# A selective-scan kernel: the softplus correction moves from GpSimd to TensorE, row statistics from VectorE to ScalarE

## The chip, the core and the metric

One core of a Trainium2 chip runs the whole kernel. It has four compute engines that run side by side, each with its own instruction stream: TensorE (PE: matmuls, with PEld for the weight loads), VectorE (DVE), ScalarE (ACT) and GpSimd (POOL); SyncE (SP) here only issues DMAs. Engines wait for each other by semaphores. Inside an engine the order is fixed: an instruction that waits holds up all behind it. SBUF is the on-chip memory, PSUM the memory into which TensorE writes; GpSimd doesn't touch PSUM in this kernel. The metric is the device time of one execution in microseconds; a run of this kernel can tell about 0.2% from no change.

## The reference, cut to what matters

Input x is 8 batches of 512 tokens of width 256. The first half is a selective scan (a Mamba block) with residual and norms; the second half is a shared and a routed feed-forward layer with 8 experts.

```
x   = x + layernorm(ssm(layernorm(x)))
h   = layernorm(x) * norm_w + norm_b ;  h = h @ in_proj_w.T        # 512 channels
h   = silu(conv4(h))                    # 4 taps along time
dt  = softplus(proj[..., :1] @ dt_proj_w.T + dt_proj_b)            # proj = h @ x_proj_w.T
state = exp(A * dt_t) * state + B_t * x_t      # 16 states per channel, 512 steps of time
y   = sum over states of state * C_t  + D * x_t
out = silu(y) @ out_proj_w.T + x
x   = x + layernorm(shared_ffn(n) + routed_ffn(n)),  n = layernorm(x)
```

The softplus is computed as max(z, 0) + log(1 + u) with u = exp(-|z|). With w = 1 + u rounded, and then w - 1, the kernel has the rounded u in the tile lt; log(1 + lt) is compared with lt. The difference lt - log(1 + lt), called the loss, plus a margin of 2e-9, is cut at (0.707 u)^2 by a minimum. The time step is dt = max(z, 0) + u - minimum.

## The kernel before

**Layout.** 512 channels are 4 chunks of 128 partitions (C = 4), each with 512 tokens in the free dimension. Two chunks are a half (H = 2), so one scan works on a tile of 128 x 1024 of one state, and a batch has Q = 32 scans: 16 states for each of two halves.

**A round.** Round i (the iteration function of each engine) handles the scans of batch i, and between them, at given steps q of the 32, the front of batch i+1 (norm, input projection, convolution, Silu, projections, dt), the back of batch i-1 (output projection, residual, norms, router matmuls), and the lead of batch i+2 (the statistics of x). Nothing but the code's order of each engine and the semaphores set when a thing runs.

**A step q.** ScalarE writes the decays exp(A dt) for scan q+2 into PSUM (tile psX, two halves of 128x511, L763, ring of 2). The input product bx = x * B comes from GpSimd for even q (L500, issued four steps ahead, from B rows spread over the partitions by DMA) or from VectorE for odd q (L1078); for VectorE TensorE spreads the B row over the partitions with one matmul into the bank psB (spread_b, L1486), two steps ahead. Step 22 is an exception, its product is VectorE's. VectorE scans (L1090). GpSimd multiplies the state by C (L511, 'weigh'). TensorE sums the weighted states of step q-3 into psY (total, L1529). psB is one bank: a spread must wait until VectorE has read the one before.

**The front's dt part, by steps.** 10: ScalarE's Silu with a table load before and one behind (L660, L610), 11 to 14: projections on TensorE, the dt row on ScalarE, 14 to 17: |z|, exp, 1 + u, minus 1 on ScalarE (L673, L676, L679, L682), 18: ScalarE copies y out of PSUM (keep_y, L753). 19: the logarithm (L685). 20: GpSimd's lt minus logarithm (L516, 128x2048). 22: ScalarE's square (L688). 23 and 24: VectorE's minimum in two halves (L1039, 128x1024 each, both operands in SBUF). 25 to 28: for each chunk three matmuls by plus or minus identity add relu(z), u and the minimum in the bank psF (L1433 to L1435), and ScalarE copies the sum to dt (L694); one bank serves all, so the next sum waits for the copy.

**The back, by steps.** 15 and 17: output projection (L1451), 16 and 18: residual on VectorE (L1048), 19: router matmuls of batch i-2 (choose, L1476), 22 and 24: second residual (L1058), 25: statistics, 29 and 30: transposes (L1467). **The lead.** Step 10: VectorE takes the statistics of x of batch i+2 (L1006, four bn_stats, and L1010) into mv0; steps 29 to 31: ScalarE makes scale and bias of them and norms x. The statistics are copied at step 8 for the back of the same batch.

Before round 0 a function first_front handles batch 0 alone, and it is not changed. Round 7 has no front and no lead.

## Time and profile before

| | |
|---|---|
| time, median of 3 runs | 1411.01 us (1410.88 to 1412.58) |
| the profiled execution's own time | 1411.09 us |
| its span, first to last instruction | 1409.3 us |
| mean granted TensorE clock | 0.94 |
| PE busy | 1175.4 us (83%) |
| DVE busy | 1089.8 us (77%) |
| ACT busy | 770.9 us (55%) |
| POOL busy | 1088.4 us (77%) |

The scans run from 51.7 to about 989 us, then come the tail of the last batch, the shared layer and the routed layer. The busy shares of the table are means over all of that; the change lies in the scan stage alone, and what a piece of it is worth has to be read there, in one round. In the page's 40 slices, TensorE's granted clock is 0.8 to 0.9 of full speed in the scan stage, and 0.9 behind it.

### The profile page before, as it was taken

The numbers are of one execution on the slowest core, as the hardware profiler recorded it, in microseconds if no ns is written. First come the engines' busy times: TensorE is split into PE (matmuls) and PEld (weight loads), VectorE is DVE, ScalarE is ACT, GpSimd is POOL, SyncE is SP. The second block draws the span as 40 slices with busy tenths as digits, with TensorE's granted clock in tenths as the row PEclk, the third lists the DMA queues.
The fourth block names the chain that finished last, engine by engine and source line by source line (L and its number), as shares of the span: only waits on it lengthen the run. The fifth ranks groups of instructions, "written<-read, shape, count | busy, mean of one in ns | idle before, by whom it ended". The sixth has DMA issues, their size and how long they took to land.

```text
span 1409.3 us, 15754 instructions
## 1 busy us (share of the span) xinstructions
PE 1175.4 (83%) x4782; PEld 518.5 (37%) x4783; DVE 1089.8 (77%) x1449; ACT 770.9 (55%) x1275; POOL 1088.4 (77%) x565
## 2 busy tenths in 40 slices
PE   5667678787886987888789688788999999999996
PEld 2222223222321422322233142233556655566653
DVE  3599999999999999999999989799241115776675
ACT  5757468676876866867686686556431111111111
POOL 0489999999999999999999999999122814444553
PEclk9898899999899999989998999999999999999998
DMA  3921211240150122014015012300269522222220
GB/s 108 274 68 62 90 60 32 75 150 0 65 192 1 62 91 106 32 75 149 1 66 175 1 62 90 134 0 31 90 238 324 162 71 82 81 81 79 83 67 15
DMA packets 72075, 127.71 MB, mean 91 GB/s; under 512 B 8759, under 2 KB 48448, under 8 KB 67904
## 3 DMA queue, kind: packets, MB, share of 16 engines
q1 hardware_dynamic: 60432, 103.72, 22.2%
q0 software_dynamic: 7152, 16.81, 3.7%
q10 hardware_dynamic: 4416, 6.29, 1.3%
q8 instruction: 33, 0.54, 0.2%
q14 instruction: 42, 0.34, 0.1%
HBM read 97.79 MB, written 31.76 MB: 92 GB/s over the span
## 4 chain that ended last, share of the span: by engine, by line
PE 36%; POOL 29%; issue 15%; DVE 12%; ACT 8%; DMA 0%; POOLq 0%; ACTq 0%; SPq 0%; DVEq 0%
POOL state L511 18%; PE psX L1647 10%; POOL bx L500 9%; DVE state L1090 6%; PE psX L1582 5%; PE psY L1595 3%; PE psY L1664 2%; PE bank L1664 2%; PE psY L1529 2%; PE bank L1451 2%; POOL lt L516 2%; ACT psX L763 2%; PE bank L1486 1%; DVE bx L1078 1%; DVE acc L1025 1%
## 5 line engine op out<-in xcount | busy, mean ns | idle before, releaser
L511 POOL TENSOR_TENSOR state<-state,cbc 128x1024 f32<-128x1024 f32 x256 | 606.6, 2398 | 14.9 <-DVE state L1090 14.8
L1090 DVE TENSOR_TENSOR_SCAN state<-psX,bx 128x1024 f32<-128x1024 f32 x256 | 578.5, 2279 | 38.5 <-ACT psX L763 23.1
L763 ACT ACTIVATE psX<-dt,aneg 128x511 f32<-128x511 f32 x512 | 330.7, 679 | 199.0 <-DVE state L1090 197.6
L500 POOL TENSOR_TENSOR bx<-xh,bbc 128x1024 f32<-128x1024 f32 x120 | 291.1, 2426 | 59.5 <-DMA bbc<-bc_rows 43.1
L1529 PE MATMUL psY<-state,ident 64*64 64x512 f32 x2048 | 287.5, 654 | 20.3 <-POOL state L511 20.0
L1486 PE MATMUL bank<-prow,ident 128*128 128x512 f32 x272 | 169.9, 710 | 113.3 <-DVE bx L1078 113.3
L1078 DVE TENSOR_TENSOR bx<-xh,bank 128x1024 f32<-128x1024 f32 x136 | 162.7, 1196 | 7.7 <-PE bank L1486 7.6
L1529 PEld LDWEIGHTS psY<-state,ident 64*64 64x64 f32 x2048 | 63.9, 140 | 206.8 <-issue 126.2
L961 ACT ACTIVATE sg<-psX 128x512 f32<-128x512 f32 x39 | 23.3, 597 | 196.5 <-PE psX L1647 196.5
L1486 PEld LDWEIGHTS bank<-prow,ident 128*128 128x128 f32 x272 | 48.0, 209 | 206.9 <-DVE bx L1078 166.9
L581 POOL DMA_INDIRECT ysl<-shared_rows,idx x39 | 40.3, 1033 | 80.6 <-DVE idx L1258 75.9
L1167 DVE TENSOR_TENSOR actS<-sg,psX 128x512 f32<-128x512 f32 x28 | 19.0, 686 | 103.6 <-ACT sg L911 103.6
L1647 PE MATMUL psX<-wg,xsT 128*128 x156 | 77.2, 617 | 1.3 <-DVE xsT L1243 0.6
L1647 PE MATMUL psX<-wu,xsT 128*128 x156 | 73.3, 592 | 0.0
L1406 PE MATMUL bank<-lt,win 128*128 128x512 f32 x112 | 55.5, 618 | 15.7 <-DVE acc L1025 14.4
L590 POOL DMA_INDIRECT result<-yo,idx x39 | 40.1, 1029 | 36.8 <-DVE yo L1306 29.3
L1025 DVE SCALAR_TENSOR_TENSOR acc<-bank,cw,acc 128x511 f32<-128x511 f32 (+2 forms) x84 | 62.3, 742 | 3.3 <-ACT acc L654 1.2
L561 POOL COPY xrow<-ids 128x4 f32<-128x4 f32 x8 | 1.6, 203 | 77.6 <-issue 55.1
L1249 DVE TENSOR_TENSOR actN<-sg,psX 128x512 f32<-128x512 f32 x39 | 26.8, 688 | 44.1 <-ACT sg L961 41.6
L1451 PE MATMUL bank<-wout,yv 128*128 128x256 f32 x256 | 58.5, 381 | 2.0 <-ACT yv L709 1.9
L911 ACT ACTIVATE sg<-psX 128x512 f32<-128x512 f32 x28 | 16.5, 596 | 76.8 <-PE psX L1582 76.8
L1582 PE MATMUL psX<-xg,shg 128*128 128x512 f32 x112 | 53.1, 596 | 1.8 <-DVE actS L1167 1.8
(200 smaller groups left out, 1718.8 us busy)
## 6 DMA issues: line engine op xcount, KB each, us to landing
cbc<-bc_rows SPq DMA_DIRECT2D x32, 1024.0 KB, 5.0
bbc<-bc_rows SPq DMA_DIRECT2D x16, 1024.0 KB, 6.2
slot_in<-ao SPq DMA_DIRECT2D x1, 5011.5 KB, 35.1
xsl<-slot_in SPq DMA_DIRECT2D x39, 128.5 KB, 2.0
xin<-in_x SPq DMA_DIRECT2D x8, 512.0 KB, 4.5
xr<-in_x SPq DMA_DIRECT2D x8, 512.0 KB, 5.5
x_rows<-ao SPq DMA_DIRECT2D x8, 512.0 KB, 2.9
xn_rows<-xr SPq DMA_DIRECT2D x8, 512.0 KB, 3.2
```

What stands on the lines that cost most here:

```text
L500: nc.gpsimd.tensor_tensor(bx[q % RB][:], xh[par][:, h * CH:(h + 1) * CH], bbc[:, n // 2].unsqueeze(1).broadcast_to([P, CH, L]), ALU.mult). ...
L511: nc.gpsimd.tensor_tensor(w[:], w[:], cbc[:, n].unsqueeze(1).broadcast_to([P, CH, L]), ALU.mult).then_inc(weighted, 1)
L763: e = nc.scalar.activation(decay[q % RD][:, c, 1:L], dt[par][:, h * CH + c, 1:L], ACT.Exp, scale=aneg[:, h * CH + c, n:n + 1])
L1025: last = nc.vector.scalar_tensor_tensor(out=acc[:, c, m:L], in0=psF[:, 0:L - m], scalar=cw[:, c, TAPS - 1 - m:TAPS - m], in1=acc[:, c, m:L ...
L1078: nc.vector.tensor_tensor(bx[q % RB][:], xh[par][:, h * CH:(h + 1) * CH], psB[:].unsqueeze(1).broadcast_to([P, CH, L]), ALU.mult).then_inc ...
L1090: nc.vector.tensor_tensor_scan(st[q % RS][:].rearrange("p c t -> p (c t)"), decay[q % RD].rearrange("p c t -> p (c t)"), bx[q % RB][:].rea ...
L1451: last = nc.tensor.matmul(psF[:, (j % 2) * DIM:(j % 2 + 1) * DIM], yv[:, c, j * P:(j + 1) * P], wout[:, c], start=(c == 0), stop=(c == C - 1))
L1486: nc.tensor.matmul(psB[:], ident[:, n:n + 1].broadcast_to([P, P]), prow[par][:], start=True, stop=True).then_inc(b_bcast, 1)
L1529: done = nc.tensor.matmul(psY[o * HP:(o + 1) * HP, r], weights(half, c), src[half, c], start=first, stop=last_)
L1582: last = nc.tensor.matmul(bank, w[:, k, c * P:(c + 1) * P], xg[g % 2][:, k], start=(k == 0), stop=(k == KC - 1))
L1647: last = nc.tensor.matmul(bank, xsT[i][:, k], w[:, bass.ds(ereg[i], 1), k].rearrange("p a n -> p (a n)"), start=(k == 0), stop=(k == KC - 1))
L1664: last = nc.tensor.matmul((psF, psG)[i][:, 0:DIM], actT[i][:, c], wd[:, bass.ds(ereg[i], 1), c].rearrange("p a n -> p (a n)"), start=(c == ...
```

## The change

**Loss.** GpSimd's subtraction is gone. TensorE makes it, chunk by chunk, at steps 19, 21, 23 and 25 (LOSS_AT), in the chunk order 2, 3, 0, 1 (LOSS_ORDER): two matmuls into psB, identity by lt and minus identity by the logarithm. VectorE's minimum comes behind the scan of the same step, as four instructions of 128x512 that read psB, and each spread of B that stood at these steps now stands one step later, behind the wait for the minimum. ScalarE's logarithm moves from step 19 to 18 in two halves, the upper chunks' into the tile yv; the square is split in two (steps 19 and 21), and Relu moves from 23 to 22. The dt sums take the chunks in the new order.

**Products.** Step 22's product goes to GpSimd, which has 16 of 32 now.

**Statistics of x.** VectorE's lead is gone from the loop. ScalarE makes them with eight passes over 256 columns that sum up along the row: four sums at steps 3 to 6, the mean and the first sum of squares at step 7, three more at step 9. Each pass waits for the one before. The copy of the statistics moves from step 8 to 6.

The pieces of the diff, in the order of the file: the constants, GpSimd's subtraction, ScalarE's lead and front, VectorE's minimum and its lead in the loop, TensorE's loss and its loop.

```diff
-    BY_POOL = [q % 2 == 0 and q not in (22,) for q in range(Q)]
+    BY_POOL = [q % 2 == 0 for q in range(Q)]
+    LOSS_AT = (19, 21, 23, 25)
+    LOSS_ORDER = (2, 3, 0, 1)
...
-            def loss(f, par):
-                pool.wait_ge(soft_ready, f + 1)
-                nc.gpsimd.tensor_tensor(lt[:], lt[:], dt[par][:], ALU.subtract).then_inc(loss_ready, 1)
...
             def lead(f, par, q):
+                def row_pass(k, func, bias, dst):
+                    if k == 0:
+                        act.wait_ge(mv0_ready, f)
+                    else:
+                        act.wait_ge(row_passes, (2 * J - 1) * (f - 2) + k)
+                    nc.scalar.activation(unused[:], xin[:, k % J, :], func, bias=bias,
+                                         accum_out=dst).then_inc(mv0_ready if k == 2 * J - 1 else row_passes, 1)
+                if q in (3, 4, 5, 6):
+                    j = q - 3
+                    if j == 0:
+                        act.wait_ge(x_loaded, 16 * (f + 1))
+                    row_pass(j, ACT.Identity, 0.0, xsum[:, j:j + 1])
+                if q == 7:
+                    act.wait_ge(row_passes, (2 * J - 1) * (f - 2) + J)
+                    nc.scalar.activation(mv0[par][:, :, 0], xsum[:], ACT.Identity,
+                                         scale=-1.0 / DIM).then_inc(mean_ready, 1)
+                    act.wait_ge(mean_ready, f - 1)
+                    row_pass(J, ACT.Square, mv0[par][:, 0, 0:1], mv0[par][:, 0, 1:2])
+                if q == 9:
+                    for j in range(1, J):
+                        row_pass(J + j, ACT.Square, mv0[par][:, j, 0:1], mv0[par][:, j, 1:2])
...
+                if q == 18:
+                    act.wait_ge(lt_ready, f + 1)
+                    if not (isinstance(f, int) and f == 1):
+                        act.wait_ge(oproj_ready, 2 * (f - 1))
+                    nc.scalar.activation(yv[:, CH:C], lt[:, CH:C], ACT.Ln, bias=1.0)
+                    nc.scalar.activation(dt[par][:, 0:CH], lt[:, 0:CH], ACT.Ln, bias=1.0).then_inc(soft_ready, 1)
                 if q == 19:
-                    act.wait_ge(lt_ready, f + 1)
-                    nc.scalar.activation(dt[par][:], lt[:], ACT.Ln, bias=1.0).then_inc(soft_ready, 1)
+                    nc.scalar.activation(dt[par][:, CH:C], tmp[:, CH:C], ACT.Square, scale=HALF_ROOT).then_inc(sq_ready, 1)
+                if q == 21:
+                    act.wait_ge(loss_made, C * (f - 1) + 2)
+                    nc.scalar.activation(yv[:, CH:C], tmp[:, 0:CH], ACT.Square, scale=HALF_ROOT).then_inc(sq_ready, 1)
...
-                if q in (23, 24):
-                    h = slice(0, 2) if q == 23 else slice(2, 4)
-                    dve.wait_ge(loss_ready, f + 1)
-                    dve.wait_ge(sq_ready, f + 1)
-                    nc.vector.scalar_tensor_tensor(out=lt[:, h], in0=lt[:, h], scalar=LN_MARGIN, in1=dt[par][:, h],
+                if q in LOSS_AT:
+                    k = LOSS_AT.index(q)
+                    c = LOSS_ORDER[k]
+                    dve.wait_ge(loss_made, C * (f - 1) + k + 1)
+                    if c < CH:
+                        dve.wait_ge(sq_ready, 2 * f + 1)
+                        square = yv[:, CH + c]
+                    else:
+                        dve.wait_ge(sq_ready, 2 * f)
+                        square = dt[par][:, c]
+                    nc.vector.scalar_tensor_tensor(out=lt[:, c], in0=psB[:], scalar=LN_MARGIN, in1=square,
                                                    op0=ALU.add, op1=ALU.min).then_inc(min_done, 1)
...
-                    if do_lead:
-                        lead(i + 2, par, q)
...
+            def loss(f, par, q):     
+                k = LOSS_AT.index(q)
+                c = LOSS_ORDER[k]
+                logarithm = dt[par][:, c] if c < CH else yv[:, c]
+                pe.wait_ge(soft_ready, f + 1)
+                pe.wait_ge(dve_bx, (f - 1) * DQ + NTH_D[q + 1])
+                nc.tensor.matmul(psB[:], ident[:], lt[:, c], start=True, stop=False)
+                nc.tensor.matmul(psB[:], minus[:], logarithm, start=False, stop=True).then_inc(loss_made, 1)
...
                 for q in range(Q):
-                    if not BY_POOL[(q + 2) % Q]:
+                    if do_front and q - 1 in LOSS_AT:
+                        pe.wait_ge(min_done, 2 + C * i + LOSS_AT.index(q - 1) + 1)
+                        spread_b(i, par, q + 1)
+                    if do_front and q in LOSS_AT:
+                        loss(i + 1, 1 - par, q)
+                    elif not BY_POOL[(q + 2) % Q]:
```

TensorE before, steps 17 to 21 of a round that has all parts: the second output projection and the sum of step 14 open it; `bank<-prow` is a spread of B, `psY<-xh,dD` the skip term.

```order
L1486 MATMUL bank<-prow,ident 128x512
L1451 MATMUL bank<-wout,yv 128x256 x8
L1529 MATMUL psY<-state,ident 64x512 x8
L1486 MATMUL bank<-prow,ident 128x512
L1529 MATMUL psY<-xh,dD 64x512 x4
L1529 MATMUL psY<-state,ident 64x512 x4
L1476 MATMUL bank<-gw,xnTb 128x8 x8
L1486 MATMUL bank<-prow,ident 128x512
L1529 MATMUL psY<-state,ident 64x512 x4
L1486 MATMUL bank<-prow,ident 128x512
```

And in the changed kernel, from the spread of step 17 on (L1533 is the spread, L1524 and L1525 the loss, L1489 the output projection, L1514 the router, L1576 the sums):

```order
L1533 MATMUL bank<-prow,ident 128x512
L1489 MATMUL bank<-wout,yv 128x256 x8
L1576 MATMUL psY<-state,ident 64x512 x8
L1524 MATMUL bank<-lt,ident 128x512
L1525 MATMUL bank<-yv,minus 128x512
L1576 MATMUL psY<-xh,dD 64x512 x4
L1576 MATMUL psY<-state,ident 64x512 x4
L1514 MATMUL bank<-gw,xnTb 128x8 x8
L1533 MATMUL bank<-prow,ident 128x512
L1576 MATMUL psY<-state,ident 64x512 x4
L1524 MATMUL bank<-lt,ident 128x512
```

The spread of step 21 stood ahead of the skip term and the router; now the two loss matmuls stand there, and the spread has gone behind the router.

TensorE before, from the last spread of the minimum's stretch: the spread of step 27, the sum of step 22 and the first dt sum.

```order
L1486 MATMUL bank<-prow,ident 128x512
L1529 MATMUL psY<-state,ident 64x512 x4
L1433 MATMUL bank<-acc,ident 128x512
L1434 MATMUL bank<-tmp,ident 128x512
L1435 MATMUL bank<-lt,minus 128x512
L1529 MATMUL psY<-state,ident 64x512 x4
L1433 MATMUL bank<-acc,ident 128x512
L1434 MATMUL bank<-tmp,ident 128x512
L1435 MATMUL bank<-lt,minus 128x512
L1486 MATMUL bank<-prow,ident 128x512
```

And now (L1471 to L1473 are the dt sums):

```order
L1524 MATMUL bank<-lt,ident 128x512
L1525 MATMUL bank<-dt,minus 128x512
L1576 MATMUL psY<-state,ident 64x512 x4
L1471 MATMUL bank<-acc,ident 128x512
L1472 MATMUL bank<-tmp,ident 128x512
L1473 MATMUL bank<-lt,minus 128x512
L1533 MATMUL bank<-prow,ident 128x512
L1576 MATMUL psY<-state,ident 64x512 x4
L1471 MATMUL bank<-acc,ident 128x512
```

The loss stands in the place of the spread of step 27, and that spread is between the first and the second dt sum.

VectorE before, from scans 19 and 20 to scan 24 (L1078 the products, L1039 the first half of the minimum):

```order
L1090 SCALAR_TENSOR_TENSOR state<-psX,bx 128x1024 x2
L1078 TENSOR_TENSOR bx<-xh,bank 128x1024
L1090 SCALAR_TENSOR_TENSOR state<-psX,bx 128x1024
L1078 TENSOR_TENSOR bx<-xh,bank 128x1024
L1090 SCALAR_TENSOR_TENSOR state<-psX,bx 128x1024
L1078 TENSOR_TENSOR bx<-xh,bank 128x1024
L1058 TENSOR_TENSOR ao<-bank,xr 128x512
L1090 SCALAR_TENSOR_TENSOR state<-psX,bx 128x1024
L1039 SCALAR_TENSOR_TENSOR lt<-lt,dt 128x1024
L1090 SCALAR_TENSOR_TENSOR state<-psX,bx 128x1024
```

And now, from scan 19 on (L1129 the scans, L1117 the products, L1078 the minimum of one chunk):

```order
L1129 SCALAR_TENSOR_TENSOR state<-psX,bx 128x1024
L1078 SCALAR_TENSOR_TENSOR lt<-bank,dt 128x512
L1129 SCALAR_TENSOR_TENSOR state<-psX,bx 128x1024
L1117 TENSOR_TENSOR bx<-xh,bank 128x1024
L1129 SCALAR_TENSOR_TENSOR state<-psX,bx 128x1024
L1078 SCALAR_TENSOR_TENSOR lt<-bank,dt 128x512
L1129 SCALAR_TENSOR_TENSOR state<-psX,bx 128x1024
L1117 TENSOR_TENSOR bx<-xh,bank 128x1024
L1097 TENSOR_TENSOR ao<-bank,xr 128x512
L1129 SCALAR_TENSOR_TENSOR state<-psX,bx 128x1024
L1078 SCALAR_TENSOR_TENSOR lt<-bank,yv 128x512
```

A minimum stands behind scan 19 already, between it and scan 20, and of the three products in a row that of step 22 is gone. Scans are printed as SCALAR_TENSOR_TENSOR here.

## Rows read from the trace of the kernel before

**Rows 1.** Busy time by engine in round 4: us, busy (x instructions), PEclk, DMA share, GB/s.
```profile
528.90:646.00 117.10, 96.53 (x423) 34.81 (x418) 109.88 (x95) 85.28 (x142) 113.88 (x48) 0.91 0.22 77
```

**Rows 2.** Timeline, DVE: start, us, line, out<-in, [idle before <-releaser]; two scans 0.
```profile
528.90 2.29 DVE L1090 TENSOR_TENSOR_SCAN state<-psX,bx 128x1024 f32<-128x1024 f32 x1 [1.46 <-ACT psX L763]
...
646.03 2.29 DVE L1090 TENSOR_TENSOR_SCAN state<-psX,bx 128x1024 f32<-128x1024 f32 x1 [1.25 <-ACT psX L763]
```

**Rows 3.** Groups by line: xcount | busy us, mean ns | idle before, releaser.
```profile
L511 POOL TENSOR_TENSOR state<-state,cbc 128x1024 f32<-128x1024 f32 x256 | 606.6, 2398 | 14.9 <-DVE state L1090 14.8
...
L763 ACT ACTIVATE psX<-dt,aneg 128x511 f32<-128x511 f32 x512 | 330.7, 679 | 199.0 <-DVE state L1090 197.6
...
L516 POOL TENSOR_TENSOR lt<-lt,dt 128x2048 f32<-128x2048 f32 x7 | 31.8, 4540 | 0.0
...
L1025 DVE SCALAR_TENSOR_TENSOR acc<-bank,cw,acc 128x511 f32<-128x511 f32 (+2 forms) x84 | 62.3, 742 | 3.3 <-ACT acc L654 1.2
...
L631 ACT ACTIVATE lt<-xin,nmr,rstd 128x256 f32<-128x256 f32 x32 | 17.1, 588 | 0.1
...
L1006 DVE BATCH_NORM_STATS2 bst<-xin 128x6 f32<-128x256 f32 x32 | 11.2, 414 | 3.7 <-DMA xin<-in_x 3.7
```

**Rows 4.** Timeline, POOL, steps 16 to 19 of round 4.
```profile
592.88 7.03 POOL L511 TENSOR_TENSOR state<-state,cbc 128x1024 f32<-128x1024 f32 x3
602.84 2.36 POOL L511 TENSOR_TENSOR state<-state,cbc 128x1024 f32<-128x1024 f32 x1 [2.92 <-DVE state L1090]
```

**Rows 5.** Timeline, DVE: scans 13 and 14, and the residual sum of step 16.
```profile
578.28 4.47 DVE L1090 TENSOR_TENSOR_SCAN state<-psX,bx 128x1024 f32<-128x1024 f32 x2 [0.69 <-ACT psX L763]
...
591.65 0.69 DVE L1048 TENSOR_TENSOR ao<-bank,ao 128x512 f32<-128x512 f32 x1 [2.02 <-PE bank L1451]
```

**Rows 6.** Timeline, ACT: decays of step 10, copy of y, logarithm.
```profile
569.31 1.30 ACT L763 ACTIVATE psX<-dt,aneg 128x511 f32<-128x511 f32 x2 [3.10 <-DVE state L1090]
...
599.95 1.08 ACT L753 ACTIVATE yv<-psY 128x512 f32<-128x512 f32 x2
...
604.03 1.90 ACT L685 ACTIVATE dt<-lt 128x2048 f32<-128x2048 f32 x1
```

**Rows 7.** Timeline, DVE: products of steps 21 and 25, second half of the minimum.
```profile
604.86 1.20 DVE L1078 TENSOR_TENSOR bx<-xh,bank 128x1024 f32<-128x1024 f32 x1
...
619.84 1.19 DVE L1078 TENSOR_TENSOR bx<-xh,bank 128x1024 f32<-128x1024 f32 x1
...
621.55 1.77 DVE L1039 SCALAR_TENSOR_TENSOR lt<-lt,dt 128x1024 f32<-128x1024 f32 x1
```

**Rows 8.** Timeline, PE: step 19, then the spread of step 27 and a dt sum.
```profile
599.81 1.12 PE L1486 MATMUL bank<-prow,ident 128*128 128x512 f32 x2
601.17 1.09 PE L1529 MATMUL psY<-xh,dD 64*64 64x512 f32 x8 [0.24 <-ACT yv L753]
...
603.05 1.95 PE L1476 MATMUL bank<-gw,xnTb 128*128 128x8 f32 x16
...
621.09 2.07 PE L1486 MATMUL bank<-prow,ident 128*128 128x512 f32 x2 [3.26 <-DVE bx L1078]
...
624.78 1.13 PE L1433 MATMUL bank<-acc,ident 128*128 128x512 f32 x2
```

**Rows 9.** Busy time by engine behind that idle stretch, columns as in rows 1.
```profile
621.00:625.00 4.00, 3.92 (x11) 1.03 (x12) 4.00 (x4) 0.45 (x1) 4.00 (x2) 0.57 0.37 131
```

**Rows 10.** Timeline of round 0: ACT's copy of y, DVE's first half minimum.
```profile
127.77 1.06 ACT L753 ACTIVATE yv<-psY 128x512 f32<-128x512 f32 x2
...
142.04 8.26 DVE L1039 SCALAR_TENSOR_TENSOR lt<-lt,dt 128x1024 f32<-128x1024 f32 x1 [1.13 <-ACT dt L688]
```

**Rows 11.** Round 0: landing of x, issued at 63.03; ACT's decays of step 4.
```profile
63.03 4.00 SPq L362 DMA_DIRECT2D xin<-in_x  x1
...
DMA to landing us min/median/max: 15.3/15.3/15.3
...
74.47 1.30 ACT L763 ACTIVATE psX<-dt,aneg 128x511 f32<-128x511 f32 x2 [3.11 <-DVE state L1090]
```

More of the change, by code:

```diff
@@ L123, in build @@
         mv0 = [sb(f"mv0_{i}", [P, J, 2], where=A) for i in range(2)]
+        xsum = sb("xsum", [P, J], where=A)
+        unused = sb("unused", [P, DIM], BF16, where=A)
         mv = [sb(f"mv{i}", [P, J, 2], where=A) for i in range(3)]
@@ L240, in build @@
         mv0_ready = sem("mv0_ready")
+        row_passes = sem("row_passes")
+        mean_ready = sem("mean_ready")
         mv_ready = [sem(f"mv_ready{i}") for i in range(3)]
@@ L525, in iteration @@
                     weigh(i, q)
-                    if do_front and q == 20:
-                        loss(i + 1, 1 - par)
             for q in range(0, RB, 2):
@@ L759, in decays @@
                     act.wait_ge(scanned, i * Q + q - RD + 1)
-                if n == 0:
-                    act.wait_ge(dt_ready, C * i + CH * (h + 1))
+                if n == 0 and isinstance(i, int) and i == 0:
+                    act.wait_ge(dt_ready, CH * (h + 1))
+                elif n == 0:
+                    act.wait_ge(dt_ready, C * (i + 1))
                 for c in range(CH):
@@ L1423, in front @@
                 if q in (25, 26, 27, 28):
-                    c = q - 25
+                    k = q - 25
+                    c = LOSS_ORDER[k]
                     pe.wait_ge(relu_ready, f + 1)
-                    pe.wait_ge(min_done, 2 * f + c // 2 + 1)
-                    if c:
-                        pe.wait_ge(dt_ready, C * f + c)
+                    pe.wait_ge(min_done, 2 + C * (f - 1) + k + 1)
+                    if k:
+                        pe.wait_ge(dt_ready, C * f + k)
                     else:
```

30 lines of the change are left out of this document (17 added, 13 removed).

## The prediction, made before the changed kernel had run

> **What bounds the kernel now.** I read the page first, then the busy times of one round, then the timelines of VectorE, ScalarE and TensorE through it. A round is one pass of the 32-step loop of one batch; a step q is one scan of a state. Round 4 runs from scan 0 at 528.90 to the next scan 0 at 646.03 us, 117.1 us [rows 2]. In it GpSimd is busy 113.9, VectorE 109.9, TensorE 96.5 and ScalarE 85.3 us, at a granted clock of 0.91 [rows 1]. GpSimd looks like the bound, and the change takes work from it. Its own sum: 32 weightings and 15 products at 2.31 us from start to start (three in a row take 7.03 [rows 4]; the mean of one is 2.40 with the overlap [rows 3]) are 108.6, the 128x2048 subtraction 4.5 [rows 3], so 113.1, 4 less than the round. And it waits: at step 19 for 2.92 us, for the scan [rows 4]. A bound engine doesn't wait once a round. I therefore take VectorE's row of work for what sets the round, with the waits in it for ScalarE and TensorE: 0.69 us before scan 13 for its decays, 2.02 before the residual sum of step 16 for TensorE [rows 5], 1.25 before the next scan 0 [rows 2]. The question is then what becomes of those waits and whether new ones come in.
>
> **The statistics of x leave VectorE (step 10).** Four bn_stats at 0.41 us [rows 3] and the small operations behind them are about 1.7 us. What comes next on VectorE is scans 11 and 12, the product of step 13 and scan 13, and scan 13 waits for ScalarE, which has since the end of scan 10 made decays 12, loaded a table, done both Silus and loaded the table back, from 569.31 on [rows 6]; the old 0.69 us wait is the end of that. With the 1.7 us gone, scan 13 still starts at 578.3 and the wait is 2.4. The same chain runs on through the dt row, the projections and the output projection to the residual sum at 591.65, 22.3 us behind scan 10, with 2.02 us of waiting left over there too [rows 5, 6]. So I cost this part at zero, not at -1.7 (bounds -1.7 and 0).
>
> **Its replacement on ScalarE.** Eight passes over 256 columns, each waiting for the one before: 0.59 us each by the pass of the same shape over the same tile [rows 3], 4.7 us and two small ones. No row has such a pass with an accumulated sum; the bounds are the row itself and, as an estimate, twice it, 1.2. I take 0.6, the nearer row. They stand in steps 3 to 7 and 9, where ScalarE idles before its decays: 3.10 us before those of step 10 [rows 6], where three passes go in (1.9), and 199 us over the kernel's 512 decay halves, nearly all waiting for a scan [rows 3]. Zero, up to +0.5 a round at 1.2 us each. One exception: x must now be there at step 3. In round 0 its load is issued at 63.03 and lands 15.3 us later, at 78.3, beside the 5 MB of zeros; ScalarE's next decays were at 74.47 [rows 11] and have the second convolution tap behind them, for which VectorE is then late. About +3 us, once.
>
> **The product of step 22 goes to GpSimd.** VectorE saves 1.2 to 1.4 us. GpSimd takes the 2.3 in the gap before step 19's scan [rows 4], which covers it.
>
> **The loss goes from GpSimd to TensorE.** This is the dear part. TensorE, in order, now does at step 19: two matmuls of 512 columns into psB, the weighted sum of step 16, the router's matmuls; and only at step 20, after VectorE's minimum has read psB, the spread of B for step 21. Before, that spread was first of all. When can the first matmul start? Both logarithms must be done. ScalarE's copy of y out of PSUM, which stays ahead of them, ends at 601.0 [rows 6]; two half-size logarithms of 0.95 each (half of the whole one's 1.90, same group) end at 602.9. TensorE has been free since about 599.9, where it now has the spread [rows 8]. Two matmuls at about 1.0 (an identity matmul at the high clock is 1.13 alone, and overlaps with the next [rows 8]): 605.0. Scan 19 ended at 602.7, as GpSimd's start behind it tells [rows 4], so VectorE stands 2.4 us. The minimum, from PSUM, is 0.66 start to start (0.74 each by the convolution's form [rows 3]). Behind the two matmuls TensorE has the sum of step 16 with its skip term, 1.9 (601.17 to 603.05), the router 1.95 and the spread 1.0 [rows 8], to 610.0. The product of step 21, which started at 604.86 [rows 7], starts at 610.1: +5.2. From there VectorE goes product, scan, minimum (the loss of the next chunk runs under the scan), so its row to the product of step 25 is: saved 1.4 (step 22) and the old first minimum with its wait 1.7, added two minima 1.3. That product starts at 623.2 or 623.3 instead of 619.84 [rows 7]: +3.4.
>
> Then the last loss and the four sums. Behind the product of step 25 TensorE had one spread and a weighted sum, 3.7 us from 621.09 to the first of the dt sums at 624.78, at the low clock [rows 8]; now two matmuls and that sum, 3.0 at the high one. That is -0.7. The spread of step 27 now stands between the first and the second dt sum: +1.0. ScalarE copies each sum, and the last copy, the transposes and the norm's small operations release the decays of the next scan 0; this is what the 1.25 us wait is the end of [rows 2]. VectorE's shorter second minimum (1.77 to 0.66, [rows 7]) lies beside it. Net +0.3. A round at the high clock: +3.4 +0.3, with 0.2 to 0.4 of semaphore times, **+4.1**.
>
> **The clock.** In rows: TensorE idled 3.26 us before 621.09, and its next matmul took 2.07 instead of 1.13 [rows 8]; the granted clock in that stretch was 0.57, so mostly 1.2 GHz [rows 9]. In the changed kernel it idles from 599.9 to 602.9, nearly as long, ahead of matmuls for which VectorE stands. Cold they cost +2.0, and the sum and router behind them +1.3: +3.3. I take half of that. The Trainium skill, TensorE: Matmul & The Clock Gate, section HAM oscillation, says that an array left without work for long enough goes back to the low clock, so that what follows the wait starts slow, every round. That rule counts the whole of it.
>
> **Sum.** Rounds 2 to 6: 5 x 4.1 = 20.5. Round 1 has no router matmuls ahead of the spread: 4.1 - 2.0 = 2.1. Round 0: its first minimum took 8.26 us after 1.13 of waiting [rows 10], where a later one took 1.77 [rows 7], with GpSimd busy beside both; the new form reads one operand from PSUM, as the convolution does, whose 84 instructions have a mean of 0.74 [rows 3], so that goes; but the first loss waits till 132.8 (copy of y to 128.8 [rows 10], 1.9, 1.95) against scan 19's end at 127.4. By the same walk the step 25 scan is about 6 us earlier and the dt chain gives back 3; with x's 3 us: 0. Round 7 has no front: it lost the step 22 product from VectorE (-1.4), GpSimd gains 2.3 but enters with less in arrears: -1. Together +21.6 warm; six rounds of half the clock's 3.3 are +10: about +31 less a little. Against the profiled execution's 1411.09 us (span 1409.3, 1.8 around it, and the median of the runs 1411.01) that is **1441 us**.
>
> **The rivals.** (a) *GpSimd is the bound after all* (faster). By its row a round goes from 113.1 and two delays of 1.0 by the old minima to 48 x 2.31 = 110.9, -4.2; seven rounds -29, +2.3 in the last: 1384. For it: 113.9 busy of 117.1 [rows 1]; the Trainium skill, SBUF — State Buffer, section SBUF: two separate sides, adds that a VectorE operation with two SBUF inputs takes a port pair that GpSimd shares, so the old minima, and not the new ones, would hold it up. Against it: the 2.92 us wait [rows 4], and that no VectorE wait names GpSimd. It needs the loss to be ready when scan 19 ends, 2.4 us earlier than I find; part of it, with the step 22 product and stats saved and psB's turn hidden, would give 1390 to 1405. (b) *Cold TensorE* (slower than forecast): 3.3 at the first loss in six rounds and as much as 2.9 before the dt sums (3.26 us of idle led to that before): 21.6 + 20 + 17 = +58, 1469. This is also where the skill's clock rule points: the first of the two alone gives 1411 + 21.6 + 20 = 1453. (c) *The moves cancel*: the router and the weighted sum turn out to lie under VectorE's scans, and +5.2 shrinks to about the 2.4 of the wait, while 1.2, 1.0 and 0.7 come back: -0.5 to +1 a round, 1408 to 1416. (d) *The statistics don't hide*: 1.2 us passes push the decays before both Silus and the whole chain by 0.5 to 1 us a round, +4 to +7 on any of the others.
>
> **How the numbers follow.** Forecast with its neighbours (1424 to 1456): 0.54. Cold (b), above 1456: 0.19. (c): 0.08, half of it within 0.2%, which is 2.8 us and about what runs of this kernel can tell. (a): 0.19. So faster by over 0.2% has 0.20, within 0.04, slower 0.76. The range should leave out at most 2 in 10: from 1400 (a part of (a) stays out) to 1468 (the end of (b)). The likeliest case alone: 1424 to 1456.
>
> **What would show it.** Right: no bn_stats of x on VectorE, and scan 13 waiting about 2.4 us for ScalarE; VectorE idle 2 to 4 us before the first of the four minima, released by TensorE, and again before the product of step 21; GpSimd idle several us more in every round; 121 to 124 us from scan 0 to scan 0 in rounds 2 to 6. Wrong: the first minimum starting right behind scan 19; scan 13 moving up with the statistics gone, which would give 1.7 us a round that I give nothing for; GpSimd without a gap and rounds of 111 to 114 us, which is rival (a); or rounds of 117.

## The result, and the profile after

The changed kernel takes **1433.9 us** (median of 4 runs, 1432.7 to 1435.2) against 1411.6 (4 runs, 1410.9 to 1412.6): ratio **1.0157, 95% interval 1.0144 to 1.0170**. It is slower, as forecast, by 22 us in place of 30. The profiled execution took 1433.3 us.

The page of the changed kernel, its span, its busy times and the shares of its chain:

```profile
span 1431.2 us, 16057 instructions
...
PE 1203.3 (84%) x4878; PEld 533.3 (37%) x4879; DVE 1060.0 (74%) x1401; ACT 796.9 (56%) x1393; POOL 1064.5 (74%) x566
...
PE 48%; ACT 20%; DVE 20%; issue 10%; DMA 1%; DVEq 0%; ACTq 0%; POOLq 0%; POOL 0%; SPq 0%
```

The chain is the work that ended last, followed back from the end of the kernel. In the page of the kernel before its shares were:

```profile
PE 36%; POOL 29%; issue 15%; DVE 12%; ACT 8%; DMA 0%; POOLq 0%; ACTq 0%; SPq 0%; DVEq 0%
```

GpSimd and VectorE have each lost work (24 and 30 us), and the kernel is slower. In the chain GpSimd's share is 0% where it was 29%. Round 4, columns as in [rows 1]:

```profile
539.90:661.60 121.70, 100.06 (x443) 36.92 (x440) 106.62 (x87) 89.73 (x161) 111.23 (x49) 0.94 0.22 75
```

It is 4.6 us longer than before [rows 1], with 3.3 us less on VectorE and 2.6 less on GpSimd. So waits grew. Where, the starts of the scans tell, in us from the round's scan 0, read from VectorE's timeline of both traces (the columns are scans):

| round 4 | 13 | 17 | 19 | 20 | 21 | 23 | 25 | 28 | 31 | next 0 |
|---|---|---|---|---|---|---|---|---|---|---|
| before | 49.4 | 63.4 | 71.6 | 73.8 | 77.3 | 84.9 | 94.3 | 104.0 | 113.6 | 117.1 |
| after | 49.2 | 63.2 | 71.4 | 77.6 | 83.7 | 90.4 | 97.1 | 107.4 | 118.2 | 121.7 |

To scan 19 nothing has moved. Scan 20 is 3.8 later, scan 21 is 6.4 later; by scan 25 it has given back 3.6 of that, and 1.8 come back on before scan 0. VectorE's timeline at these places (start, us, line, out<-in, and in brackets the idle before it and its releaser):

```profile
589.12 4.47 DVE L1129 TENSOR_TENSOR_SCAN state<-psX,bx 128x1024 f32<-128x1024 f32 x2 [2.12 <-ACT psX L793]
...
602.49 0.69 DVE L1087 TENSOR_TENSOR ao<-bank,ao 128x512 f32<-128x512 f32 x1 [2.01 <-PE bank L1489]
...
611.34 2.26 DVE L1129 TENSOR_TENSOR_SCAN state<-psX,bx 128x1024 f32<-128x1024 f32 x1
...
616.90 0.69 DVE L1078 SCALAR_TENSOR_TENSOR lt<-bank,dt 128x512 f32<-128x512 f32 x1 [3.30 <-PE bank L1525]
617.51 2.28 DVE L1129 TENSOR_TENSOR_SCAN state<-psX,bx 128x1024 f32<-128x1024 f32 x1
...
622.19 1.22 DVE L1117 TENSOR_TENSOR bx<-xh,bank 128x1024 f32<-128x1024 f32 x1 [2.40 <-PE bank L1533]
...
661.63 2.29 DVE L1129 TENSOR_TENSOR_SCAN state<-psX,bx 128x1024 f32<-128x1024 f32 x1 [1.24 <-ACT psX L793]
```

Scan 13 and the residual sum of step 16 start where they started, 0.69 [rows 5] having become 2.12 before the first of them. The two new waits, 3.30 for the first loss and 2.40 for the spread behind it, are 5.7 us. The wait for scan 0 is the old one [rows 2]. ScalarE at steps 18 and 19: the copy of y, then the two logarithms, which end at 613.76:

```profile
610.79 1.08 ACT L781 ACTIVATE yv<-psY 128x512 f32<-128x512 f32 x2
611.76 1.06 ACT L710 ACTIVATE yv<-lt 128x1024 f32<-128x1024 f32 x1
612.70 1.06 ACT L711 ACTIVATE dt<-lt 128x1024 f32<-128x1024 f32 x1
```

TensorE from there:

```profile
608.77 1.95 PE L1576 MATMUL psY<-state,ident 64*64 64x512 f32 x16
613.81 1.25 PE L1524 MATMUL bank<-lt,ident 128*128 128x512 f32 x2 [3.09 <-ACT dt L711]
614.85 1.91 PE L1525 MATMUL bank<-yv,minus 128*128 128x512 f32 x2
616.69 1.76 PE L1576 MATMUL psY<-xh,dD 64*64 64x512 f32 x8
618.28 1.03 PE L1576 MATMUL psY<-state,ident 64*64 64x512 f32 x8
619.24 1.95 PE L1514 MATMUL bank<-gw,xnTb 128*128 128x8 f32 x16
621.05 1.10 PE L1533 MATMUL bank<-prow,ident 128*128 128x512 f32 x2
```

TensorE idles 3.09 us until the logarithms end; the second loss matmul and the skip term take 1.91 and 1.76 where the same kinds take 1.02 and 1.09 elsewhere; then the router, and the spread last. The clock granted in such a stretch differs from round to round. Busy times by engine, the PEclk third from the end, of the six us from 73 us behind scan 0, in rounds 1, 3 and 4:

```profile
250.15:256.15 6.00, 5.69 (x16) 1.94 (x20) 2.04 (x3) 2.49 (x4) 2.35 (x1) 0.50 0.75 220
492.20:498.20 6.00, 4.67 (x28) 2.07 (x28) 3.65 (x3) 3.44 (x5) 2.54 (x2) 1.00 0.68 203
612.90:618.90 6.00, 5.09 (x20) 1.51 (x20) 2.70 (x3) 3.02 (x4) 2.35 (x1) 0.72 0.69 217
```

It is 1.00 in round 3 (and 5), 0.72 in round 4 (and 2 and 6), where part of the stretch went at 1.2 GHz, and 0.50 in round 1, where all of it did. The idle time ahead of it is 3.1 us in all of these rounds. Round 1 has both loss matmuls slow, and its skip term took 1.99:

```profile
250.46 2.07 PE L1524 MATMUL bank<-lt,ident 128*128 128x512 f32 x2 [3.09 <-ACT dt L711]
252.32 1.92 PE L1525 MATMUL bank<-yv,minus 128*128 128x512 f32 x2
```

In round 0, where TensorE idled 9.9 us, the two took 2.07 and 1.92 as well. VectorE's wait for the first loss follows the clock: 3.96 us in round 1, 3.26, 3.30 and 2.66 in rounds 2, 4 and 6, 2.35 in rounds 3 and 5.

GpSimd, off the path, now waits more: 0.96 and 3.83 us at steps 19 to 21, where before it waited 2.92 once [rows 4]. Summed over the kernel (the waits: waiter, releaser, us, times, longest), its products waited for VectorE 16.4 us before and now:

```profile
POOL bx L507 <- DVE state L1129: 63.3, 41, 5.7
```

By rounds, scan 0 to scan 0, in us:

| round | 0 | 1 | 2 | 3 | 4 | 5 | 6 |
|---|---|---|---|---|---|---|---|
| before | 125.3 | 116.7 | 116.9 | 118.3 | 117.1 | 118.1 | 115.8 |
| after | 125.2 | 120.2 | 121.9 | 120.7 | 121.7 | 120.5 | 119.8 |
| difference | -0.1 | +3.5 | +5.0 | +2.4 | +4.6 | +2.4 | +4.0 |

The sum is +21.8. In rounds 2 to 5 the differences alternate, and so do the rounds of both kernels: before, 3 and 5 are the long ones, and after, 2 and 4. In the kernel before, the low clock reached further into the dt sums in round 3 than in round 4 (same columns, 9.5 us from 94.5 us behind scan 0):

```profile
505.10:514.60 9.50, 9.50 (x30) 3.10 (x22) 9.27 (x14) 3.68 (x6) 9.50 (x5) 0.82 0.35 132
623.40:632.90 9.50, 9.50 (x38) 2.91 (x30) 9.27 (x13) 4.58 (x11) 9.50 (x5) 0.94 0.37 136
```

There the kernel before loses its time too: from scan 28 to scan 31 it takes 10.7 and 10.8 us in rounds 3 and 5, and 9.4 and 9.6 in rounds 2 and 4. In the changed kernel the clock over the dt sums is 1.00 in all rounds. Round 7 to the start of its last scan is 106.7 in both, and what follows from there takes 422.7 before and 422.6 after.

### The profile page after: what moved, and what is told of

Its sections match the earlier page's. It is cut to its first block, busy times and chain, and to the rows that moved or that the text cites. A ratio compares the mean times of both kernels' runs of the same rounds, so it can differ in the third digit from the quotient of the medians.

```text
span 1431.2 us, 16057 instructions
## 1 busy us (share of the span) xinstructions
PE 1203.3 (84%) x4878; PEld 533.3 (37%) x4879; DVE 1060.0 (74%) x1401; ACT 796.9 (56%) x1393; POOL 1064.5 (74%) x566
## 4 chain that ended last, share of the span: by engine, by line
PE 48%; ACT 20%; DVE 20%; issue 10%; DMA 1%; DVEq 0%; ACTq 0%; POOLq 0%; POOL 0%; SPq 0%
PE psX L1699 10%; DVE state L1129 10%; ACT psX L793 5%; PE psY L1576 5%; PE psX L1634 5%; PE bank L1533 3%; DVE bx L1117 3%; DVE acc L1060 3%; PE psY L1647 3%; PE psY L1716 2%; PE bank L1716 2%; PE bank L1471 2%; PE bank L1456 2%; PE bank L1473 2%; PE bank L1472 2%
## 5 line engine op out<-in xcount | busy, mean ns | idle before, releaser
L1129 DVE TENSOR_TENSOR_SCAN state<-psX,bx 128x1024 f32<-128x1024 f32 x256 | 579.4, 2281 | 50.7 <-ACT psX L793 33.1
L518 POOL TENSOR_TENSOR state<-state,cbc 128x1024 f32<-128x1024 f32 x256 | 599.3, 2365 | 14.7 <-DVE state L1129 14.7
L507 POOL TENSOR_TENSOR bx<-xh,bbc 128x1024 f32<-128x1024 f32 x128 | 303.4, 2371 | 106.6 <-DVE state L1129 63.3
L1576 PE MATMUL psY<-state,ident 64*64 64x512 f32 x2048 | 273.9, 629 | 1.2 <-POOL state L518 1.2
L1533 PE MATMUL bank<-prow,ident 128*128 128x512 f32 x256 | 152.5, 680 | 70.5 <-DVE bx L1117 68.6
L1117 DVE TENSOR_TENSOR bx<-xh,bank 128x1024 f32<-128x1024 f32 x128 | 153.4, 1198 | 22.7 <-PE bank L1533 22.5
L1576 PEld LDWEIGHTS psY<-state,ident 64*64 64x64 f32 x2048 | 63.2, 137 | 178.1 <-issue 148.5
L1533 PEld LDWEIGHTS bank<-prow,ident 128*128 128x128 f32 x256 | 44.1, 201 | 149.3 <-DVE bx L1117 99.3
L1524 PE MATMUL bank<-lt,ident 128*128 128x512 f32 x56 | 33.0, 672 | 48.4 <-ACT dt L711 28.5
L1489 PE MATMUL bank<-wout,yv 128*128 128x256 f32 x256 | 58.5, 381 | 1.0 <-ACT yv L737 0.9
```

The source lines that it names most:

```text
L507: nc.gpsimd.tensor_tensor(bx[q % RB][:], xh[par][:, h * CH:(h + 1) * CH], bbc[:, n // 2].unsqueeze(1).broadcast_to([P, CH, L]), ALU.mult). ...
L518: nc.gpsimd.tensor_tensor(w[:], w[:], cbc[:, n].unsqueeze(1).broadcast_to([P, CH, L]), ALU.mult).then_inc(weighted, 1)
L1117: nc.vector.tensor_tensor(bx[q % RB][:], xh[par][:, h * CH:(h + 1) * CH], psB[:].unsqueeze(1).broadcast_to([P, CH, L]), ALU.mult).then_inc ...
L1129: nc.vector.tensor_tensor_scan(st[q % RS][:].rearrange("p c t -> p (c t)"), decay[q % RD].rearrange("p c t -> p (c t)"), bx[q % RB][:].rea ...
L1489: last = nc.tensor.matmul(psF[:, (j % 2) * DIM:(j % 2 + 1) * DIM], yv[:, c, j * P:(j + 1) * P], wout[:, c], start=(c == 0), stop=(c == C - 1))
L1533: nc.tensor.matmul(psB[:], ident[:, n:n + 1].broadcast_to([P, P]), prow[par][:], start=True, stop=True).then_inc(b_bcast, 1)
```

## The experiments

Theory: VectorE's row of work, with the waits in it for ScalarE and TensorE, sets the round; the loss at step 19 stands in that row, and nothing else of the change costs or gives anything there. Rivals: GpSimd's total sets it; or the pieces taken from VectorE had been worth something, and a larger cost hides that. Ratios are against the kernel before. Round times are from each run's one profiled execution.

### One part alone, on the kernel before

**The statistics of x alone** (ScalarE's eight passes in, the bn_stats out, as in the change's diff).

> The kernel before with only the statistics of x moved to ScalarE. Theory (VectorE's row with the ScalarE chain that starts behind scan 10 sets the round): the 1.7 us that leave step 10 come back as a wait before scan 13 (0.69 to 2.4 us); each round keeps its length, and round 0 grows by up to 3 us because ScalarE waits for x: 1411 to 1415. Rival (VectorE's busy time is what counts): 1.7 us in six rounds, 1401.

1408.4 us (10 runs, 1406.6 to 1414.2), 0.9987 [0.9973, 1.0000]. Rounds 1 to 6 are 117.1, 117.6, 118.2, 117.4, 118.0 and 115.7, 704.0 in sum against 702.9: as before, although VectorE has 1.7 us less in each. Scan 13 of round 4 waits 2.12 here too:

```profile
581.77 4.47 DVE L1121 TENSOR_TENSOR_SCAN state<-psX,bx 128x1024 f32<-128x1024 f32 x2 [2.12 <-ACT psX L789]
```

So this part is worth zero in the loop, as costed. Round 0 was 127.5, +2.2, for the later x. The runs lie in two groups, about 1408 (six) and 1414 (four); the profiled one, with its one stall in round 0, is of the upper. What parts them isn't shown. The 6 us between them are near what such a stall costs (below), but no run of the lower group has a profile.

**Step 22's product alone.**

```diff
-    BY_POOL = [q % 2 == 0 and q not in (22,) for q in range(Q)]
+    BY_POOL = [q % 2 == 0 for q in range(Q)]
```

> The kernel before with only the product of step 22 moved to GpSimd. Theory: VectorE's 1.4 us turn into a longer wait before the first half of the minimum, which hangs on GpSimd's subtraction and ScalarE's square; GpSimd's 2.3 us go into its gap before step 19: 1409 to 1412. Rival 1 (GpSimd is the bound): 2.3 us in eight rounds, 1429. Rival 2 (VectorE's work is the bound without the chain): -1.4 in eight, 1400.

1428.9 us (4 runs), **1.0125** [1.0108, 1.0142]: a miss, and a large one. The number is the one that "GpSimd is the bound" gave, but the rounds are not: four of rounds 1 to 6 take 117.2 to 118.7, and rounds 3 and 6 take 125.6 and 123.9. Those two are 15.4 of the 18 us, round 0 is another 2.6. In rounds 3 and 6 the first half of the minimum (L1039, both operands in SBUF) is stuck:

```profile
501.34 8.26 DVE L1039 SCALAR_TENSOR_TENSOR lt<-lt,dt 128x1024 f32<-128x1024 f32 x1 [2.48 <-ACT dt L688]
...
862.90 8.25 DVE L1039 SCALAR_TENSOR_TENSOR lt<-lt,dt 128x1024 f32<-128x1024 f32 x1 [3.29 <-ACT dt L688]
```

GpSimd beside the first of them:

```profile
501.50 2.42 POOL L500 TENSOR_TENSOR bx<-xh,bbc 128x1024 f32<-128x1024 f32 x1
503.81 4.71 POOL L511 TENSOR_TENSOR state<-state,cbc 128x1024 f32<-128x1024 f32 x2
```

VectorE began at 501.34, GpSimd's next instruction at 501.50; GpSimd ran three instructions in a row, to 508.52, and VectorE ended at 509.60, 1.1 us behind them. The 14 of its kind take 1.34 us at the least and 1.77 in the median. The kernel before has one such stall, in round 0 [rows 10], and this one has that too. In a round without it the meeting is the same, but it is GpSimd whose instruction is the longer one, 3.36 us in place of some 2.4 (the kernel before, round 1):

```profile
263.86 1.36 DVE L1039 SCALAR_TENSOR_TENSOR lt<-lt,dt 128x1024 f32<-128x1024 f32 x1 [0.64 <-ACT dt L688]
...
264.06 3.36 POOL L500 TENSOR_TENSOR bx<-xh,bbc 128x1024 f32<-128x1024 f32 x1
```

The start doesn't tell the two cases apart. In the kernel before, in the one with the statistics alone and in this one there are 21 first halves of the minimum; all began 0.25 to 0.28 us ahead of the end of the GpSimd instruction then running, and 5 were stuck. What decides isn't in these traces. The change's minima read one operand from PSUM, and none is stuck, here or in the eight kernels below that are made from it, 252 minima in all (source line: count, min/median/max in ns, first and last start):

```profile
L1078 DVE SCALAR_TENSOR_TENSOR lt<-bank,dt x14: 666/678/692, 136.9 to 867.5; 128x512 f32<-128x512 f32 x14
L1078 DVE SCALAR_TENSOR_TENSOR lt<-bank,yv x14: 657/666/669, 149.5 to 882.6; 128x512 f32<-128x512 f32 x14
```

In the undisturbed rounds scan 23 was 1.3 us earlier and scan 25 where it had been: with step 22's product gone, the minimum waits for ScalarE's square instead (its waits for it went from 3.8 us to 18.0). So the product is worth nothing to the old order, and with it gone the stall strikes in two more rounds.

**Most of GpSimd's subtraction left out** (only the first token of each chunk is subtracted, in 0.22 us in place of 4.54).

```diff
-    nc.gpsimd.tensor_tensor(lt[:], lt[:], dt[par][:], ALU.subtract)
+    nc.gpsimd.tensor_tensor(lt[:, :, 0:1], lt[:, :, 0:1], dt[par][:, :, 0:1], ALU.subtract)
```

> The kernel before with GpSimd's subtraction done for one column of each chunk only (the rest of it is left out), 4.5 us less GpSimd work a round. Theory: GpSimd isn't the bound; only VectorE's 0.3 us wait for the minimum goes, and in round 0 a part of its 8.3 us minimum: 1402 to 1410. Rival (GpSimd is the bound): 4.2 to 4.5 us in seven rounds, 1380 to 1382.

1408.1 us (9 runs), 0.9975 [0.9964, 0.9985]. GpSimd has 4.3 us less to do in every round, and rounds 1 to 6 are 117.1, 118.8, 117.6, 118.2, 117.4 and 116.4, as before. **GpSimd's total is not the bound**, at 97% busy. The gain is round 0's, 118.6 instead of 125.3 (rounds 1 to 6 are 2.6 longer in sum): the stall has gone, and the longest of the 14 minima is 2.5 us:

```profile
L1039 DVE SCALAR_TENSOR_TENSOR lt<-lt,dt x14: 1875/2010/2500, 140.9 to 851.6; 128x1024 f32<-128x1024 f32 x14
```

### Taking the cost of the loss apart, on the changed kernel

**The router's matmuls from step 19 to 18**, into TensorE's idle time ahead of the loss.

```diff
-                    if q == 19 and i >= 2:
+                    if q == 18 and i >= 2:
```

> The changed kernel with the router matmuls at TensorE's step 18, in its idle time before the first loss, and not between the loss and the spread for step 21. Theory: 1.9 us come back in each of rounds 2 to 6, 1424 to 1426. Rival (the time goes elsewhere: the statistics, the dt sums or GpSimd): 1432 to 1435.

1425.7 us (4 runs), 1.0098 [1.0081, 1.0115]: 8.2 us less than the changed kernel by the medians, as expected. Rounds 2 to 6 are 120.2, 119.9, 119.8, 119.8, 117.4: 1.5 less in the mean, of the 1.9 expected. In these rounds TensorE's idle time before the loss is now 1.2 us, and still the low clock is behind it in all but round 3. In round 5:

```profile
731.66 2.07 PE L1524 MATMUL bank<-lt,ident 128*128 128x512 f32 x2 [1.21 <-ACT dt L711]
```

**Router at 18, and the first two losses released by the first of the two logarithms.**

```diff
-                    nc.scalar.activation(yv[:, CH:C], lt[:, CH:C], ACT.Ln, bias=1.0)
+                    nc.scalar.activation(yv[:, CH:C], lt[:, CH:C], ACT.Ln, bias=1.0).then_inc(soft_ready, 1)
...
-                pe.wait_ge(soft_ready, f + 1)
+                pe.wait_ge(soft_ready, 2 * f if c >= CH else 2 * f + 1)
```

> The changed kernel with the router at step 18 and the first two losses released by the first of the two half logarithms. Theory: the first loss starts 0.95 us earlier in seven rounds, 6 to 7 us off the 1425.7 of the router edit alone: 1418 to 1420. Rival (the wait for the logarithm isn't on the path): 1425 to 1427.

1418.9 us (4 runs), 1.0050 [1.0033, 1.0066]: another 6.8, as expected, for a logarithm that ends 0.95 earlier seven times. By rounds it isn't even: 2.6 and 1.8 less in rounds 1 and 2, where the clock is also higher than with the router alone (0.72 for 0.50, 1.00 for 0.72), 1.1, 0.9 and 0.9 less in rounds 3 to 5, where it is the same, and 1.0 more in round 6, for a cause that stays open. Rounds 3 to 5 show that TensorE's start of the first loss is on the path one for one; that the whole came out at 6.8 is luck in part.

**The logarithms ahead of the copy of y at step 18**, the router left at 19 (the diff is what moves: the call of the front).

```diff
+                    if do_front and q == N + SUM_LAG - 1:
+                        front(i + 1, 1 - par, q)
...
-                    if do_front:
+                    if do_front and q != N + SUM_LAG - 1:
```

> The changed kernel with ScalarE's two half logarithms ahead of its copy of y in step 18. Theory: the first loss starts 1.0 to 1.1 us earlier, the sum of step 16 may start as much later as before but not later than the loss's end: 0.8 to 1.1 us in seven rounds, 1426 to 1429. Rival (the logarithm isn't what TensorE and VectorE wait for): 1434, or later because of the copy of y.

1419.3 us (4 runs), 1.0062 [1.0045, 1.0079]: a gain of 14.6, about twice the expected 5 to 8. Rounds 2 to 5 are 118.9, 119.2, 119.3 and 119.4, all alike. TensorE's idle time before the loss is 1 us shorter, and in rounds 2 to 6 its matmuls then run at the high clock's durations (here round 4):

```profile
604.27 1.12 PE L1526 MATMUL bank<-lt,ident 128*128 128x512 f32 x2 [2.02 <-ACT dt L711]
605.23 1.02 PE L1527 MATMUL bank<-yv,minus 128*128 128x512 f32 x2
606.18 1.09 PE L1578 MATMUL psY<-xh,dD 64*64 64x512 f32 x8
```

In these rounds the clock's price is gone too: rounds 3 and 5, at the high clock in both kernels, gain 1.5 and 1.1, rounds 2, 4 and 6 gain 3.0, 2.4 and 2.5. Round 1 keeps the low clock (0.74 over its six us, the second loss matmul at 1.91), also behind 2.0 us of idle time. The first minimum now waits 2.35 us for ScalarE's square, and no longer for TensorE:

```profile
607.48 0.69 DVE L1080 SCALAR_TENSOR_TENSOR lt<-bank,dt 128x512 f32<-128x512 f32 x1 [2.35 <-ACT dt L713]
```

**Logarithms first and router at 18.**

> The logarithms ahead of the copy of y, and the router at step 18. Theory: with the logarithms first, the first minimum waited 2.35 us for ScalarE's square and the product of step 21 only 0.65 us more for the spread, so the router's 1.9 us are worth 0.65 in five rounds: 1415 to 1417. Rival (the two edits add up, -8.2 on 1419.3): 1410 to 1412.

1415.8 us (8 runs), 1.0030 [1.0019, 1.0041]. The two gains don't add (they would give 1411), as the theory had it: with the square late, a router that is early helps only the product behind the minimum.

**And the first square at step 18 too**, ahead of the copy of y.

```diff
-                if q == 19:
+                if q == 18:
```

> The same with the first square in step 18 too, ahead of the copy of y. Theory: the first minimum then waits for TensorE's two matmuls alone, 1.4 instead of 3 us behind scan 19, while the copy of y and with it the sum of step 16 come 2 us later, behind the loss: 1 to 1.6 us in seven rounds, 1405 to 1411. Rival (the copy of y holds up the sums and the spread as much as is won): 1415 to 1419.

1412.8 us (10 runs), 1.0005 [0.9991, 1.0019]: it undoes the loss, somewhat short of what was expected. Rounds 2 to 6 are 117.6, 118.8, 117.2, 117.6 and 115.5, and the first minimum's wait is TensorE's again, 1.27 us in rounds 2, 4 and 5. Round 3 has the low clock (0.72) and waits 2.25.

**All four losses two steps later**, with the second square at 23.

```diff
-    LOSS_AT = (19, 21, 23, 25)
+    LOSS_AT = (21, 23, 25, 27)
...
-                if q == 21:
+                if q == 23:
```

> The changed kernel with the four losses at steps 21, 23, 25 and 27 (and the second square at 23) in place of 19, 21, 23 and 25. The logarithms are then done long before the first loss, and the spread for step 21 is ahead of the router again. Theory (the first loss's place is what costs): the product of step 25 is 5 us earlier in the round than in the changed kernel; behind it the dt sums are some 2 us later, since the last loss now stands between them; a round of 118 to 119 us and 1411 to 1416. Rival (the loss on TensorE costs wherever it stands, 16 us of matmuls in a filled engine): 1430 to 1436.

**1405.9 us** (5 runs), **0.9962** [0.9948, 0.9976]: 28 us under the changed kernel, and faster than both. It was expected at 1411 to 1416, with rounds of 118 to 119. From round 3 on the first minimum waits for nothing, and neither does the product behind it. In this kernel's round 4 (scan 0 at 530.5):

```profile
605.34 0.67 DVE L1078 SCALAR_TENSOR_TENSOR lt<-bank,dt 128x512 f32<-128x512 f32 x1
605.92 2.28 DVE L1129 TENSOR_TENSOR_SCAN state<-psX,bx 128x1024 f32<-128x1024 f32 x1
608.12 1.20 DVE L1117 TENSOR_TENSOR bx<-xh,bank 128x1024 f32<-128x1024 f32 x1
...
621.01 2.28 DVE L1129 TENSOR_TENSOR_SCAN state<-psX,bx 128x1024 f32<-128x1024 f32 x1
...
628.30 0.69 DVE L1078 SCALAR_TENSOR_TENSOR lt<-bank,yv 128x512 f32<-128x512 f32 x1 [1.42 <-PE bank L1525]
...
632.95 1.22 DVE L1117 TENSOR_TENSOR bx<-xh,bank 128x1024 f32<-128x1024 f32 x1 [1.76 <-PE bank L1533]
```

Scan 25 is at 90.5 (621.01), 3.8 us ahead of the kernel before. The last loss then stands among the dt sums, VectorE waits 1.42 and 1.76, and of the 3.8 nearly all is spent: rounds 1 to 6 are 116.5, 118.4, 117.5, 116.8, 117.3 and 115.6. The 5.2 us by which the profiled span is shorter than before are mostly round 0's (121.0 instead of 125.3, no stall). The columns of [rows 1] for its round 4:

```profile
530.50:647.30 116.80, 96.03 (x440) 35.91 (x440) 106.39 (x88) 89.21 (x160) 110.89 (x49) 0.97 0.22 77
```

The same work as the changed kernel's in 4.9 us less; TensorE is busy 4.0 less for the same kinds of matmuls, at 0.97 instead of 0.94.

**That, with the passes over x at steps 5, 6, 8, 9 and 24.**

> The late losses together with the row passes in steps 5, 6, 8, 9 (sums) and 24 (mean and squares), so that round 0 doesn't wait for x at step 3. Theory: 2 to 3 us in round 0 below the late losses alone, and in the other rounds at most 0.5 either way: 1408 to 1414. Rival (the x wait is hidden, or the squares at step 24 delay decays): the same time as the late losses alone, or above it.

1405.2 us (4 runs), 0.9957 [0.9940, 0.9974]. Round 0 went from 121.0 to 119.9; the rest can't be told from the kernel with late losses alone.

**Late losses, and the statistics back on VectorE at step 10.**

> The late losses (steps 21 to 27) with the statistics of x back on VectorE at step 10. Theory (the statistics hide in the wait before scan 13 in this kernel too): rounds 1 to 6 as without them, round 0 without its 2.7 us wait for x: 1402 to 1407. Rival (VectorE's busy time counts): 1.7 us in six rounds, 1414 to 1417.

1405.0 us (4 runs), 0.9947 [0.9930, 0.9964]. Rounds 1 to 6 are the same six numbers as with the passes on ScalarE. So moving the statistics is worth nothing in the new order either. Round 0 was to lose its wait for x and didn't get shorter, 121.1 for 121.0: in the kernel with the passes the wait costs 0.9 us more by scan 10, and by scan 13 nothing is left of it.

## Why the prediction was right in its sign, and where it was off

**What bounds.** Not GpSimd's total: the subtraction cut shows it. Not VectorE's total either: the statistics alone and back show that. What is left, and what each edit of the loss's place then moved, is VectorE's row with its waits. The evidence that the prediction had, one wait of 2.92 us of the "bound" engine [rows 4], pointed the right way.

**Statistics and passes.** Zero, as costed; scan 13 waits 2.12 (forecast 2.4). A pass was costed at 0.59 to 1.2, and taken as 0.6. The trace has the pass and, as an instruction of its own, the reading of the sum:

```profile
L642 ACT ACTIVATE unused<-xin x24: 399/404/418, 78.5 to 688.2; 128x256 bf16<-128x256 f32 x24
L642 ACT ACTIVATION_READ_ACCUMULATOR unused<-xin x24: 185/189/192, 78.8 to 688.5; 128x1 f32 x24
...
L642 ACT ACTIVATE unused<-xin,mv x24: 492/507/509, 90.3 to 700.4; 128x256 bf16<-128x256 f32 x24
```

0.59 and 0.70 together: the nearer end was right. Round 0 lost 2.9 us by scan 10 to the later x (forecast 3), of which 2.1 are left at scan 19: ScalarE idles 6.82 for its landing.

```profile
78.51 0.42 ACT L642 ACTIVATE unused<-xin 128x256 bf16<-128x256 f32 x1 [6.82 <-DMA xin<-in_x]
```

**The loss at step 19.** The walk to the product of step 21 was right. VectorE was to stand 2.4 us before the first minimum, and in rounds 3 and 5, at the high clock, it stands 2.35; the product was to start 5.2 later, and starts at 81.0 there against 75.9 in rounds 2 and 4 before, 5.1 later. Taking these same rounds on both sides (120.56 after, the mean of 3 and 5; 117.02 before, of 2 and 4), the price of a round is 3.5, against a forecast of 4.1. Its two parts were less well placed: scan 25 is 1.5 late (forecast 3.4), and from scan 25 to the next scan 0 another 2.0 is lost (forecast 0.3 and the semaphores). There ScalarE's decays for scans 29 and 30 are late now, behind the copies of the dt sums:

```profile
651.40 2.29 DVE L1129 TENSOR_TENSOR_SCAN state<-psX,bx 128x1024 f32<-128x1024 f32 x1 [0.75 <-ACT psX L793]
654.50 2.29 DVE L1129 TENSOR_TENSOR_SCAN state<-psX,bx 128x1024 f32<-128x1024 f32 x1 [0.81 <-ACT psX L793]
```

The two errors nearly cancel, which is luck. Rounds 2 to 6 sum to 18.4 for 20.5; round 1 is +3.5 for 2.1, round 0 is -0.1 for 0, round 7 is 0 for -1. Rounds 2 to 6 were to take 121 to 124 us; they take 119.8 to 121.9, and three of them lie below that band. That it is the loss and nothing else is shown by the two ways of taking the cost back: later (28 us), or earlier with its inputs (21 us).

**The clock is the term that failed.** "Cold they cost +2.0, and the sum and router behind them +1.3: +3.3. I take half of that": +10 over six rounds. (All terms sum to 31.6, of which the forecast took 30.) Measured, it costs a round about 1.3 (121.83, the mean of rounds 2 and 4, against 120.56). In rounds 2 and 4 only the second loss matmul (0.9) and the skip term (0.7) were slow; the second half of the sum, 1.03, and the router, 1.95, were not, so the 1.3 for these was too much. Rounds 3 and 5 paid nothing. Round 1 paid more, 2.9 us of slower matmuls; there the clock is the likely cause of the 1.4 by which it is over its forecast. And the term took only what the clock costs and not what it gives back: the kernel before paid 1.2 in rounds 3 and 5, where it had a low clock over the dt sums, and the changed one doesn't. As an estimate from these rounds, 1.4 for round 1 and three times 1.3 for rounds 2, 4 and 6, less two times 1.2, is +2.9, in place of +10. Without any clock term the sum was 1432.7, against 1433.9. That it came so near is luck in part, since the price at the high clock was forecast 0.6 too dear in each of five rounds, and that covers the clock's 2.9. The Trainium skill, TensorE: Matmul & The Clock Gate, section HAM oscillation, has an idle array fall back to the low clock, so that each wait is followed by a slow start. Here the length of the wait doesn't tell: 3.1 us of idle time had a low clock behind it in rounds 1, 2, 4 and 6 and not in 3 and 5, 2.0 us (the logarithms first) in round 1 and not in 2 to 6, and 1.2 us (the router early) in four of rounds 2 to 6.

**What the prediction didn't see.** It gave the stuck minimum of round 0 back as a thing that "goes", and took it for one of that round. Small edits elsewhere bring or remove it: one in the kernel before, two more with only step 22's product moved, none with the subtraction cut. No stall was seen with the new form of the minimum, in nine kernels; no run has that form alone in the old order, so that the form is the reason is argued and not shown. The Trainium skill, SBUF — State Buffer, section SBUF: two separate sides, lets the two engines share a port pair, which the one that starts first holds for its whole instruction while the other waits. The traces agree in which form waits (8.26 with both operands in SBUF, at most 0.69 with one in PSUM), and in that now the one engine waits and now the other; but the stuck minimum waited for three instructions of GpSimd and not for one.

**Left open:** what parts the two groups of runs of the kernel with the statistics alone, and why the clock alternates from round to round, before and after. One run of the kernel before was at 1404.3, 8 us under the median of the 17 in its series, which is about what it would be without its one stall; it has no profile, so this is a guess. Also open is what decides whether a minimum is stuck.
